# Causal stage of a four-layer attention and feed-forward stack: turning the weights by ordinary products, the sign of the row maximum on ScalarE, other planned durations

## What is computed

```
dot    = q @ k^T                         # per head, 512 x 512
vals   = |q|^2 + |k|^2
scores = dot*dot / (vals - 2*dot + 1e-6) + causal mask
attn   = softmax(scores)                 # over keys
out    = (attn @ v) @ w_out + b_out
```

## Time and profile before

| | before |
|---|---|
| median of three runs | 5253.66 us |
| profiled execution, own time | 5240.19 us |
| its span | 5238.2 us |
| PE busy | 4802.2 us (92%) |
| DVE busy | 3440.7 us (66%) |
| ACT busy | 2581.4 us (49%) |
| POOL busy | 2332.9 us (45%) |

### The profile page before, as it was taken

How to read it: one execution, slowest core, us unless ns; L and a number is a source line. 1 busy time by engine, 2 the same in 40 slices (tenths; PEclk the granted TensorE clock), 3 DMA queues, 4 the chain that set the end, 5 groups by cost and what they waited for, 6 DMA issues and landing times.

```text
span 5238.2 us, 66473 instructions
## 1 busy us (share of the span) xinstructions
PE 4802.2 (92%) x23008; PEld 2828.5 (54%) x23008; DVE 3440.7 (66%) x8032; ACT 2581.4 (49%) x5577; POOL 2332.9 (45%) x2331
## 2 busy tenths in 40 slices
PE   7878888999999999999999999999799999999997
PEld 4444445655555555555555555545455555555564
DVE  4554566666666666468888888878766666666653
ACT  4443444444444444356666666666544444444442
POOL 1111244544544454344555555555544544545441
PEclk9999999999999999975666666757899999999998
DMA  2000000000000000000000000000000000100000
GB/s 63 9 5 9 21 5 11 3 5 3 21 7 26 11 7 13 18 8 1 5 5 5 1 9 5 5 13 5 26 5 3 3 5 19 30 11 17 15 15 21
DMA packets 50974, 60.82 MB, mean 12 GB/s; under 512 B 11848, under 2 KB 43216, under 8 KB 50640
## 3 DMA queue, kind: packets, MB, share of 16 engines
q1 hardware_dynamic: 50640, 56.58, 3.5%
HBM read 35.61 MB, written 12.58 MB: 9 GB/s over the span
## 4 chain that ended last, share of the span: by engine, by line
PE 74%; DVE 15%; issue 4%; ACT 3%; POOL 3%; DMA 1%; SPq 1%; POOLq 0%; DVEq 0%; ACTq 0%
PE wide L694 51%; PE o_ps L694 10%; PE wide L697 6%; PE turn_ps L697 5%; DVE prob L1227 2%; DVE x_n L1101 1%; DVE st L1234 1%; POOL rn L1397 1%; DMA shifted<-resid 1%; DVE pt L1253 1%; DVE prob L1214 1%; SPq L1455 1%; PE turn_ps L694 1%; DVE w_down L1214 1%; ACT pt L1064 1%
## 5 line engine op out<-in xcount | busy, mean ns | idle before, releaser
L1427 POOL TENSOR_SCALAR prob<-prob,st 128x256 f32<-128x256 f32 (+1 forms) x1024 | 521.4, 529 | 972.5 <-DVE st L1240 972.2
L694 PE MATMUL wide<-w_in,x_t 128*128 128x512 f32 (+1 forms) x1792 | 850.5, 621 | 4.6 <-DVE w_up L1199 1.8
L694 PE MATMUL o_ps<-pt,v 128*64 128x256 f32 (+2 forms) x5632 | 646.9, 376 | 119.7 <-DVE pt L1253 63.9
L694 PE MATMUL wide<-x_t,w_up 128*128 128x512 f32 (+1 forms) x1536 | 698.9, 601 | 16.8 <-DVE k_t L1161 11.4
L1064 ACT ACTIVATE pt<-turn_ps 128x512 f32<-128x512 f32 x384 | 229.3, 597 | 850.4 <-PE turn_ps L697 850.4
L694 PEld LDWEIGHTS o_ps<-pt,v 128*64 128x64 f32 (+1 forms) x5632 | 391.2, 142 | 397.1 <-issue 186.1
L694 PE MATMUL wide<-hid 16*128 16x128 f32 (+7 forms) x2048 | 560.9, 662 | 41.7 <-DVE w_up L1199 27.7
L697 PE MATMUL turn_ps<-ident,prob 128*128 128x128 f32 x2816 | 466.1, 285 | 126.6 <-ACT pt L1064 122.6
L1035 ACT ACTIVATE prob<-prob,st 128x256 f32<-128x256 f32 (+1 forms) x1024 | 478.9, 472 | 189.8 <-DVE st L1227 189.7
L694 PEld LDWEIGHTS wide<-w_in,x_t 128*128 128x128 f32 x1792 | 350.2, 205 | 387.2 <-issue 379.2
L697 PEld LDWEIGHTS turn_ps<-ident,prob 128*128 128x128 f32 x2816 | 315.2, 142 | 417.9 <-issue 234.4
(11 more groups left out here) (137 smaller groups left out, 8187.6 us busy)
## 6 DMA issues: line engine op xcount, KB each, us to landing
kept<-resid SPq DMA_DIRECT2D x16, 512.0 KB, 2.6
x_n<-kept SPq DMA_DIRECT2D x16, 512.0 KB, 3.3
shifted<-resid SPq DMA_DIRECT2D x32, 224.0 KB
w_in<-in_f_wqkv SPq DMA_DIRECT2D x4, 1536.0 KB, 6.3
w_up<-in_f_w SPq DMA_DIRECT2D x4, 1364.0 KB, 6.1
resid<-in_x SPq DMA_DIRECT2D x8, 512.0 KB, 8.2
out<-resid SPq DMA_DIRECT2D x8, 512.0 KB, 2.9
w_down<-in_f_w SPq DMA_DIRECT2D x4, 640.0 KB
```

What stands on the lines that cost most here:

```text
L694: return eng.matmul(out, lhsT, rhs, start=start, stop=stop, skip_group_check=True)
L1427: last = eng.tensor_scalar(pr[:, local_span(t)], pr[:, local_span(t)], sm[:, 8 + t:9 + t], 1.0, ALU.mult, ALU.mult)
```

## The change

Three edits, all in stage b. `turn_a` and `turn_b` call `mm` with the weights as the stationary and the identity as the moving operand, where they called `tr`. The sign change moves from the end of `bmul` on DVE to the head of `exp` on ACT, where it waits for `bmul`, writes the same `st` columns and raises the same semaphore, for which `exp` then waits. Nine entries of `B_COST` get other numbers, and with them the planner's order and its choice of PSUM buffers can come out otherwise.

```
-B_COST = {"bclip": (0.15, 0.27), "bnum": (0.1, 0.27), "bguess": (0.25, 0.54), "bclose": (0.2, 0.6), "bmul": (0.6, 0.55),
-          "exp": (0.25, 0.26), "turn_a": (0.05, 0.14), "turn_b": (0.05, 0.14), "pt_a": (0.12, 0.135),
-          "pt_b": (0.12, 0.135), "mix": (0.1, 0.25), "mask": (0.8, 0.0)}
+B_COST = {"bclip": (0.15, 0.27), "bnum": (0.1, 0.22), "bguess": (0.2, 0.47), "bclose": (0.2, 0.6), "bmul": (0.5, 0.63),
+          "exp": (0.45, 0.26), "turn_a": (0.05, 0.16), "turn_b": (0.05, 0.16), "pt_a": (0.06, 0.12),
+          "pt_b": (0.12, 0.135), "mix": (0.1, 0.28), "mask": (0.85, 0.0)}
...
-                        last = tr(ps[:, to + kb * P:to + (kb + 1) * P],
-                                  prob[SLOTS[u, i]["prob"]][:, at + kb * P:at + (kb + 1) * P])
+                        last = mm(ps[:, to + kb * P:to + (kb + 1) * P], prob[SLOTS[u, i]["prob"]][:, at + kb * P:at + (kb + 1) * P],
+                                  ident[:, :], True, True)
...
                     exp_tables()
+                    act.wait_ge(S["bmul"], nth("bmul", u, i))
+                    eng.activation(sm[:, 0:2], sm[:, 8:10], ACT.Copy, scale=-1.0).then_inc(S["neg"], 1)
                     act.wait_ge(S["neg"], nth("bmul", u, i))
...
                     last.then_inc(S["bmul"], 1)
-                    dve.wait_ge(S["bmul"], o)
-                    eng.tensor_scalar(sm[:, 0:2], sm[:, 8:10], -1.0, None, ALU.mult).then_inc(S["neg"], 1)
```

## The result

The changed kernel takes 5173.66 us (median of 4 runs, 5154.67 to 5187.88) against 5252.14 for the kernel before beside it: a ratio of 0.9848, 95% interval 0.9811 to 0.9884. A second series gave 5165.73 and 0.9830 (0.9808 to 0.9853). So it is 80 to 90 us faster, well clear of noise, inside the stated range of 4985 to 5265 and 59 us above the forecast of 5115. The first median lies 4 us outside the forecast's own range (5025 to 5170) and on the number of the rival "the clock rises, the step hardly shortens" (5175). The profiled execution takes 5169.19 us, 71.0 less than that of before.

The account below looks back on a forecast made before the run. Stage b was taken as held by a PE hardly ever idle at about half clock. Products' cost and a clock of 0.84 took 140 us off, sign and order nought: 5240.2 to 5100, plus 13.5, said as 5115; range 4985 to 5265.

Parts of the forecast that it names:

- the clock rises, the step hardly shortens: Rival, 17%: the chain DVE, ACT, POOL, DVE, ACT through three buffers paces stage b; 5175 us.
- the forecast's own reason: Stage b: turns made into products raise PE's clock, so the PE-held stage takes 1300 us, 140 less than 1440.
- The clock: Stage b: mean clock rises from 0.66 to 0.84, within 0.74 to 0.95, through longer runs of 128 x 128 work.
- the run of turns before the rise at 2466: Stage b: 3.0 us of turns preceded this clock rise; eight blocks as products, some 3.5 us, would exceed it.
- The products: Stage b: 1280 turned blocks cost 218 instead of 109 ns each at full clock, adding 140 us of PE.
- the 158 ns with the weight load in sight: Products' upper end: 49 ns of weight load showing in each record, a block 2 x 158 ns, +265 us.
- From PE's busy time to the stage: Stage b: PE's 1028 us at full clock becomes 1224 busy at 0.84; with idle time 1300, break-even at 0.76.
- The sign: Stage b: DVE loses 141.4 us or part, ACT gains 81; on the path nought within 0.2 us a step.
- The order: Stage b, new planned durations: nought, with PE's 95 us of idle time the most to win or lose.
- PE's idle time: Stage b: 95 us now, nearly all waits for DVE and ACT; DVE gives some back, so 1319 becomes 1300.

Follow-up runs that it names:

- the doubled transposes: Kernel before with each turned block transposed twice into the same place, in place of a product: 5234.83 us, ratio 0.9973.
- PE relieved off the turns (`bdot`): Kernel before with `bdot` computing only the first 128 columns of each step, so that scores are other ones: 5185.73 us, ratio 0.9877.
- the shortened `bclose`: Changed kernel with `bclose` multiplying only 128 columns a step instead of 256 to 1024, so that scores are other ones: 4985.76 us, ratio 0.9493.

## Why the prediction was right, and where it was not

The time fell in the range and on the forecast side, but the forecast's own reason is not what made it faster: that the number came out so near was luck. The rival at 5175 is hit no better: its 78 us come from the step length of the half-clock stretch and not from the sign or the order, and with products alone nothing was gained.

- *The clock.* Foreseen 0.84, within 0.74 to 0.95; measured 0.85. The cause was right in the main: longer runs of 128 x 128 work, transposed or multiplied, gave 0.82 and 0.84 alone. But sign and order raised it too, to 0.70 and 0.71 alone and 0.75 together, for which the prediction had no term. The turns of four blocks took 3.78 us at half clock where some 3.5 was foreseen, and the run of turns before the rise at 2466 was 2.8 us by rows 4 and 5, not 3.0. The Trainium skill, "TensorE: Matmul & The Clock Gate", Part 4: PE-mode transpose, says that the full clock doesn't engage for transposes, since they don't count as PE being busy in the same way; the doubled transposes (0.84) disagree, and the measurement decides.
- *The products.* Foreseen 109 ns a record at full clock; the sixteen above stand 124 ns apart, where eight transposes have 1.02 us to the next work (2672.41 to 2673.43), 128 each. So a block costs twice as much and not four times, and the 158 ns with the weight load in sight are not there. In all the products added somewhat more than the 140 us: busy time times clock is 888 us before, 1055 with products alone and 1043 in the changed kernel. PE busy 1224 foreseen, 1227 measured: at 0.85 the sum would have given 1209. The Trainium skill, "Perfetto Trace Analysis", Optimizing Tensor Performance, Transposes, advises to do a transpose as a transpose and not as a standard matmul. By the runs that advice costs nothing here: order and sign with transposes are as fast.
- *From PE's busy time to the stage.* This step failed: "PE's busy time ... equals the present 1345 at c = 0.76. Everything hangs on whether the clock passes that." It passed it and nothing followed: with products alone PE was busy 59 us less and the stage 3 us longer. I took 93% busy for a bound. Half-clock records are long, so PE looked full while in part it followed the others; rows 10 hinted at it (5.32 us a step at half clock, 5.65 at 0.69), and I kept that as a rival at 17%. With PE relieved off the turns (`bdot`) the stage gave back about half. That the products put their added time into the chain itself, between `mask` and `pt`, is the likely reason for the difference; no run separates it.
- *The sign.* Foreseen nought within 0.2 us a step, measured 45 to 71 us, 0.18 to 0.28 us a step. The terms were mis-sized: the ACT copy takes 198 ns, not 285, so a mean of 552 ns with a long tail up to 2321 gave way to 198, on the mean 0.35 us a step. On VectorE 96 us went, inside the foreseen 43 to 141: some of the waiting passed to the next instructions, but not all.
- *The order.* Foreseen nought within 95, measured 22 alone. I was right that the trace doesn't price it, and wrong to leave it at zero beside an idle time of 95.
- *PE's idle time.* Foreseen 76, measured 128: the first number of the trace after that speaks against the forecast's reason.

What stays open: how the 177 to 186 us of the shortened `bclose` divide between GpSimd's own time in the chain and the stretching of VectorE's instructions, and why the new order helps. No run separates either. The timelines say only that the mean `bclose` is 1.1 us shorter (1.72 to 0.60) and the way from `bclip` to the end of `mask` 1.8 us, so GpSimd's own time is not all of it.

## What to carry to other kernels

A half-clock PE that is 93% busy is no proof of a PE bound: look for a stretch at another clock, and if the time for one step is the same there, expect a faster clock to turn into waiting. Where several engines stand near 80% in strict order, price an edit by what it takes off the chain of one step, an instruction of two columns included, and read its mean and its longest, not its median. And test each part of a bundled change alone before giving the credit to the most striking one.

## What the runs showed of the hardware

- Transposes of 128 x 128 in 32-bit floats raised the granted clock like products: 0.66 before, 0.82 with products alone, 0.84 with each transposed twice. Another order of the same records gave 0.71.
- A VectorE instruction of two columns took 168 to 2321 ns, with 552 as the mean, and the same on ScalarE 186 to 214: only VectorE's was stretched. All 80 long ones (0.56 us or more) ran beside a GpSimd instruction, and 79 ended with one. With GpSimd's work cut from 746 to 458 us VectorE's own busy time fell from 1087 to 979 for the same instructions.
- Removing a stretched VectorE instruction of 141 us took 96 to 97 us off its busy time.
